# Two-layer graph network on one core: the down product's three terms in one 256-column sum, with two sets of PSUM banks

## What is computed

```
h = relu(layernorm(x));  s = h @ W.T
x1 = x + segment_sum(s[dst] * edge_weight, src)
h = relu(layernorm(x1))
g = h + segment_sum(h[src], dst)
h1 = g @ W1 + b1                      # 256 -> 1024
h1 = relu(batchnorm(h1))              # mean, variance over all rows
out = x1 + relu(h1 @ W2 + b2)         # 1024 -> 256
```

## Time and profile before

| what | value |
|---|---|
| median of 3 runs | 3991.4 us (3989.78 to 3992.15) |
| profiled execution | 3991.25 us, of which 3989.1 us from its first to its last instruction |
| mean granted clock of TensorE | 0.946 |
| TensorE busy | 3528.1 us (88%) |
| VectorE busy | 2164.4 us (54%) |
| ScalarE busy | 2165.5 us (54%) |
| GpSimd busy | 1029.7 us (26%) |

### The profile page before, as it was taken

One profiled execution on the slowest core, in us unless ns is written; L12 is line 12 of the kernel. 1 busy time (PEld: TensorE's weight loads), 2 busy tenths in 40 slices (PEclk: granted clock), 3 DMA queues, 4 the chain that ended last, 5 costly groups with the idle time before them and its releaser, 6 DMA issues.

```text
span 3989.1 us, 58593 instructions
## 1 busy us (share of the span) xinstructions
PE 3528.1 (88%) x17911; PEld 3007.3 (75%) x17911; DVE 2164.4 (54%) x5128; ACT 2165.5 (54%) x3631; POOL 1029.7 (26%) x801
## 2 busy tenths in 40 slices
PE   0477876688787689999999999999999999999999
PEld 0377776577666567778888888888888888888888
DVE  0466665476565578845555455455455555545544
ACT  0355554233322299946666656666666666665665
POOL 6288888688877700000000000000000000000000
PEclk9888888788888899999999999999999999999999
DMA  9977776577777799812212212211211221221220
GB/s 340 308 188 193 184 195 131 138 168 165 160 159 154 155 350 359 330 42 74 68 63 68 74 63 64 78 63 63 79 63 63 73 69 63 69 73 63 64 78 32
DMA packets 172581, 517.35 MB, mean 130 GB/s; under 512 B 26133, under 2 KB 78352, under 8 KB 166576
## 3 DMA queue, kind: packets, MB, share of 16 engines
q1 hardware_dynamic: 96160, 412.93, 30.0%
q0 software_dynamic: 75264, 102.81, 15.4%
q10 hardware_dynamic: 1072, 0.76, 0.1%
HBM read 361.58 MB, written 206.03 MB: 142 GB/s over the span
## 4 chain that ended last, share of the span: by engine, by line
PE 59%; POOL 19%; issue 9%; DMA 7%; ACT 5%; DVE 1%; ACTq 0%; POOLq 0%; SPq 0%; DVEq 0%
PE ps_a L1208 27%; PE ps_b L1222 18%; PE ps_b L1223 9%; POOL x_table L496 7%; POOL agg_table L496 6%; POOL arena L486 6%; DMA x_table<-in_x 4%; ACT arena L625 4%; PE ps_a L1192 2%; DMA agg_table<-arena,scatter_now 1%; DMA x_table<-arena,scatter_now 1%; ACT arena_r L643 1%; PE ps_b L1119 0%; DMA arena<-x_table,gather_ids 0%; PE ps_b L1108 0%
## 5 line engine op out<-in xcount | busy, mean ns | idle before, releaser
L1208 PE MATMUL ps_a<-arena_r 128*128 128x512 f32 (+1 forms) x4704 | 1198.3, 393 | 1.5 <-DVE arena_r L1031 1.5
L1222 PE MATMUL ps_b<-arena_r 128*128 128x512 f32 x3128 | 1138.1, 399 | 0.1
L1039 DVE TENSOR_TENSOR arena_r<-arena,arena_r 128x512 fp32r<-128x512 f32 (+1 forms) x784 | 540.2, 689 | 960.4 <-ACT arena_r L682 960.4
L677 ACT ACTIVATE arena<-ps_a,bn_bias,bn_scale 128x512 f32<-128x512 f32 (+1 forms) x784 | 607.2, 774 | 779.8 <-PE ps_a L1208 779.6
L1208 PEld LDWEIGHTS ps_a<-arena_r 128*128 128x128 f32 x4704 | 835.8, 188 | 178.7 <-ACT arena_r L668 1.9
L1223 PE MATMUL ps_b<-arena_r 128*128 128x256 f32 x3128 | 875.5, 280 | 0.0
L1222 PEld LDWEIGHTS ps_b<-arena_r 128*128 128x128 f32 x3128 | 587.8, 188 | 132.5 <-issue 0.4
L1223 PEld LDWEIGHTS ps_b<-arena_r 128*128 128x128 f32 x3128 | 590.5, 189 | 26.8
L682 ACT ACTIVATE arena_r<-arena 128x512 fp32r<-128x512 f32 (+1 forms) x784 | 495.0, 631 | 71.8 <-ACT arena L677 0.4
L1119 PE MATMUL ps_b<-arena,arena_r 128*128 128x256 f32 x1568 | 410.6, 428 | 0.0
L625 ACT ACTIVATE arena<-arena,norm_now 128x256 f32<-128x256 f32 (+1 forms) x782 | 405.2, 595 | 3.5 <-DVE norm_now L930 3.5
(11 more groups left out here) (116 smaller groups left out, 3879.2 us busy)
## 6 DMA issues: line engine op xcount, KB each, us to landing
arena<-x_table SPq DMA_DIRECT2D x291, 512.0 KB, 3.7
arena<-agg_table SPq DMA_DIRECT2D x194, 512.0 KB, 5.2
x_table<-in_x SPq DMA_DIRECT2D x10, 5000.0 KB, 32.5
agg_table<-zeros SPq DMA_DIRECT2D x40, 1250.0 KB, 5.3
out<-zeros SPq DMA_DIRECT2D x97, 512.0 KB, 6.0
arena<-in_x,gather_ids POOLq DMA_INDIRECT x196, 5.1
x_table<-arena,scatter_now POOLq DMA_INDIRECT x196, 4.0
arena<-x_table,gather_ids POOLq DMA_INDIRECT x196, 2.9
```

The source lines that it names most:

```text
L677: act.activation(hid[m % 2][:, 0:w], ps_a[:, 2 + m % 2, 0:w], ACT.Relu, scale=bn_scale[:, m:m + 1], bias=bn_bias[:, m:m + 1]).then_inc(hid ...
L1039: dve.tensor_tensor(hid_lo[m % 4][:, 0:w], hid[m % 2][:, 0:w], hid_hi[m % 4][:, 0:w].bitcast(F32), ALU.subtract).then_inc(hid_lo_ready, 1)
L1208: ins = pe.matmul(ps_a[:, 2 + m % 2, 0:w], w_part[:, kb, cols], h_part[:, kb, 0:w], start=(t == 0), stop=(t == len(terms) - 1))
L1222: pe.matmul(ps_b[0:p, r, :], hid_hi[m % 4][:, cols], w2, start=(m == 0), stop=(m == MB - 1), skip_group_check=True)
```

## The change

Each row group's sum now has 256 columns, and all three terms go into the same ones, in three matmuls of 256 columns where there was one of 512 and one of 256. Two groups share a bank. A chunk so needs two banks, and chunks take turns with two sets of two. Down block 0 waits until the sums of the chunk before the last have been read. VectorE reads the sums once, in two operations, and adds the bias; the operation that adds the second half goes, and with it a wait on VectorE's own counter. Down block 7 is no longer split: it stands whole behind up 0, and the semaphore of its first half goes.

The diff, without the declaration of the semaphore, the first increment of down_read by one before the loops, the counts of finish, and the length of VectorE's own counter in its loop (2 x LOADS to 0):

```diff
+        def node_sums(s, r):
+
+            return ps_b[:, 2 * s + r // 2, r % 2 * D:(r % 2 + 1) * D]
...
-                for half, rows in enumerate(halves(j)):
-                    if half == 0:
-                        dve.wait_ge(down_half, n + 1)
-                    else:
-                        dve.wait_ge(down_done, MB * n + MB)
-                    r0, r1 = rows[0], rows[-1] + 1
-                    chain.then(dve.tensor_tensor(out_sb[s][0:p, r0:r1, :], ps_b[0:p, r0:r1, 0:D],
-                                                 b2_bc[0:p, :].rearrange("p (a d) -> p a d", a=1).to_broadcast([p, r1 - r0, D]), ALU.add))
-                    chain.wait()
-                    dve.tensor_tensor(out_sb[s][0:p, r0:r1, :], out_sb[s][0:p, r0:r1, :], ps_b[0:p, r0:r1, D:2 * D],
-                                      ALU.add).then_inc(down_read, 1)
+                dve.wait_ge(down_done, MB * n + MB)
+                for r0, r1 in ((0, 2), (2, j)):
+                    ins = dve.tensor_tensor(out_sb[s][0:p, r0:r1, :],
+                                            ps_b[0:p, 2 * s + r0 // 2, 0:(r1 - r0) * D].rearrange("p (a d) -> p a d", d=D),
+                                            b2_bc[0:p, :].rearrange("p (a d) -> p a d", a=1).to_broadcast([p, r1 - r0, D]), ALU.add)
+                ins.then_inc(down_read, 1)
...
-            def down(n, m, half=None):
+            def down(n, s, m):
...
                 if m == 0 and not (isinstance(n, int) and n == 0):
-                    pe.wait_ge(down_read, 2 * n)
-                w2 = w2_hl[:, m, :, :].rearrange("p t d -> p (t d)")
-                for r in (range(j) if half is None else halves(j)[half]):
+                    pe.wait_ge(down_read, n)
+                for r in range(j):
                     cols = slice(r * p, (r + 1) * p)
-                    pe.matmul(ps_b[0:p, r, :], hid_hi[m % 4][:, cols], w2, start=(m == 0), stop=(m == MB - 1), skip_group_check=True)
-                    ins = pe.matmul(ps_b[0:p, r, 0:D], hid_lo[m % 4][:, cols], w2[:, 0:D], start=False, stop=(m == MB - 1), skip_group_check=True)
-                ins.then_inc(down_half if half == 0 else down_done, 1)
+                    for i, (rows, part) in enumerate(((hid_hi, 0), (hid_hi, 1), (hid_lo, 0))):
+                        ins = pe.matmul(node_sums(s % 2, r)[0:p, :], rows[m % 4][:, cols], w2_hl[:, m, part, :],
+                                        start=(m == 0 and i == 0 and r % 2 == 0), stop=(m == MB - 1 and i == 2), skip_group_check=True)
+                ins.then_inc(down_done, 1)
...
-                    down(n - 1, MB - 2)
-                    down(n - 1, MB - 1, half=0)
+                    down(n - 1, (s - 1) % LOADS, MB - 2)
                 up(n, 0)
                 if not (isinstance(n, int) and n == 0):
-                    down(n - 1, MB - 1, half=1)
+                    down(n - 1, (s - 1) % LOADS, MB - 1)
```

More of the change, by code:

```diff
@@ L257, in gnn_program @@
         hid_lo_ready = sem("hid_lo_ready")
-        down_half = sem("down_half")
         down_done = sem("down_done")
@@ L880, in _ @@
             dve.sem_inc(gram_lo, 2)
+            dve.sem_inc(down_read, 1)
             dve.wait_ge(consts_ready, 3)
@@ L1005, in read_down @@
                 dve.wait_ge(out_retired, n + 1)
-                for half, rows in enumerate(halves(j)):
-                    if half == 0:
-                        dve.wait_ge(down_half, n + 1)
-                    else:
-                        dve.wait_ge(down_done, MB * n + MB)
-                    r0, r1 = rows[0], rows[-1] + 1
-                    chain.then(dve.tensor_tensor(out_sb[s][0:p, r0:r1, :], ps_b[0:p, r0:r1, 0:D],
-                                                 b2_bc[0:p, :].rearrange("p (a d) -> p a d", a=1).to_broadcast([p, r1 - r0, D]), ALU.add))
-                    chain.wait()
-                    dve.tensor_tensor(out_sb[s][0:p, r0:r1, :], out_sb[s][0:p, r0:r1, :], ps_b[0:p, r0:r1, D:2 * D],
-                                      ALU.add).then_inc(down_read, 1)
+                dve.wait_ge(down_done, MB * n + MB)
[4 more added lines that the diff above has]
+                ins.then_inc(down_read, 1)
             def finish(n, s):
                 p, j = shape_of(n)
-                dve.wait_ge(down_read, 2 * n + 2)
+                dve.wait_ge(down_read, n + 2)
                 dve.scalar_tensor_tensor(out_sb[s % 2][0:p, 0:j, :], out_sb[s % 2][0:p, 0:j, :], 0.0, x1_in[s][0:p, 0:j, :],
@@ L1046, in main @@
                         pick_norm(n + 2, s % 2)
-            main_schedule(dve, main, loop=lambda passes, body: looped(passes, 2 * LOADS, body))
+            main_schedule(dve, main, loop=lambda passes, body: looped(passes, 0, body))
             read_down(CHUNKS - 1, (CHUNKS - 1) % 2)
@@ L1236, in main @@
                     up(n, m)
-                    down(n, m - 2)
+                    down(n, s, m - 2)
             main_schedule(pe, main)
-            down(CHUNKS - 1, MB - 2)
-            down(CHUNKS - 1, MB - 1, half=0)
-            down(CHUNKS - 1, MB - 1, half=1)
+            down(CHUNKS - 1, (CHUNKS - 1) % LOADS, MB - 2)
+            down(CHUNKS - 1, (CHUNKS - 1) % LOADS, MB - 1)
 def kernel(x, src, dst, edge_weight, L0_gnn_W, L1_gnn_W1, L1_gnn_b1, L1_gnn_gamma, L1_gnn_beta, L1_gnn_W2, L1_gnn_b2):
```

## The result

The changed kernel takes 4070.25 us (median of 4 runs, 4068.69 to 4072.71); the kernel before, run beside it, 3991.78 us. The ratio is 1.020 with a 95% interval of 1.0188 to 1.0212: 78 us slower. The forecast was 4061 us, with a range from 4018 to 4085. The profiled execution took 4072.71 us, 81.5 more than that of before; their spans are 4070.8 and 3989.1 us, 81.8 apart.

What follows compares the result with a forecast made beforehand. TensorE, busy throughout the main stage at full clock, was taken as the bound. Narrower down matmuls (+31 us) and the wait before up 0 (+39 us) added 70 us to 3991.4, giving 4061 us, range 4018 to 4085.

Steps and rivals of the forecast that it cites:

- Term 1: Main stage's down blocks: twelve 256-column matmuls take 1.435 us, 0.040 more than now; 782 x 0.040 = +31 us.
- U: The six matmuls of an up call on TensorE, read as 1.39 us.
- rival on the other side: Down blocks: a 256-column matmul costs its columns only, 0.107 us, giving 3959 us; chance 0.07.
- Term 2: Before up 0: TensorE arrives too early, waits 0.295 us plus 0.11 for the weight load; 96 x 0.405 = +39 us.
- chain: ScalarE, then VectorE's subtraction, prepare up 0's transposed h; up 0 could start at 3016.64, 0.35 us to spare before the change.
- bare weight load: At up 0: a weight load behind a wait isn't hidden, 0.11 us more a chunk.
- The slack before down 0: VectorE's low part of hidden block 0 done about 3021.7, down 0 wanting it at 3022.355: 0.65 us to spare.
- rival of a further wait: Down 0 waits too if reads or low part take 0.65 longer; up to 4130 us, chance 0.04.
- The clock: Main stage: clock expected still 1.00; rival that TensorE's pauses lower it, 4230 us, chance 0.03.
- The view of waits: Sign before up 0: TensorE waiting for VectorE's subtraction some 96 times, 0.3 us each, about 28 us in all.

Runs made afterwards that it cites:

- half of down 7 first in the new and in the old layout: New: changed kernel with half of down 7 before up 0, 4017.5 us; old: kernel before with 512-column down matmuls cut into two of 256, 4015.4 us.
- the wait halved: Changed kernel, up 0 waiting for the transposed rows' first half, then for the second before its last three matmuls: 4013.6 us, ratio 1.005.
- uneven cut: Kernel before, with the 512-column matmul of a down block cut into 384 and 128 columns: 4171.0 us, ratio 1.0444.

## Why the prediction was right, and where it was off

**The bound.** TensorE had no slack in the main stage, so nothing taken from VectorE and no wait taken from down 0 could gain. The kernels with half of down 7 first in the new and in the old layout, both at 23.40 us a chunk, show it: banks and reads are worth nothing between them.

**Term 1.** Forecast 0.040 a block and 31 us; measured 0.031 a block and 23 to 26 us (the two kernels above, and 0.25 us a chunk). Its price from the edge stage's stream, 0.1196 for a matmul of 256 columns, held: a block of twelve is 1.43 us. The term was mis-sized in both of its members by a few ns: the new block came out at 1.43, not 1.435, and the present one is 1.40 in the median over the stage, not the 1.395 that came from rounding U up to 1.39 and taking it from the pair. The rival on the other side, columns alone at 0.107, is excluded by the same rows. Whether the few ns are the price of the load or of the matmul itself was not told apart, as each narrow matmul brought both. The Trainium skill's "TensorE: Matmul & The Clock Gate", section "Back-to-back issue gap", has 109 ns for 256 columns, which gives 1.31 for the block as an estimate; the section itself says that this formula counts too little for small matmuls with loads, and the trace's 1.43 agrees with that.

**Term 2.** Forecast 0.405 a chunk and 39 us; measured 0.58 a chunk, 96 x 0.58 = 55 us (53 to 57 by the medians of the changed kernel and of those with the order restored or the wait halved). The mechanism was right: chain, arrival of TensorE at 2.30 us after the transposes, and the row of waits. The step that failed in size is the one "From the end of a VectorE result to TensorE's start takes 0.05": here it took 0.24. It was taken from a place where no instruction of the sequencer stands in the way; before up 0 there are two, and the order shown ahead of the prediction has two ISA rows there. With one it is 0.14. The bare weight load was forecast at 0.11 and is 0.09 (1.48 against 1.39). So 0.295 + 0.11 became 0.49 + 0.09.

The two sizes missed in opposite ways, some 6 us too many in the one and 16 too few in the other. That the sum of 70 came within 9 us of the measured 78 is in part luck.

**The slack before down 0.** Forecast 0.65 to spare on VectorE; the changed kernel has 3023.63 - 3023.04 = 0.59, of which some 0.5 can be used, and doubling the reads turned it into a wait of 0.67. The rival of a further wait was so the right thing to fear, and the kernel with wide matmuls in the new order ran into it.

**The clock.** The granted clock was 1.00 in every stretch of the main stage, with pauses of about 0.5 us in 24. The section "A second HAM failure mode: psum-queue depth-cycling" of that page of the Trainium skill tells of a kernel in which short idle times between groups of matmuls made the clock go up and down; no row here shows that.

**The view of waits.** It gave 29.8 us in 89 rows, near the 28 forecast, while the loss was over 50, so this agreement is an accident: a record of a matmul runs on for some 0.16 us after the next could start, so a short hole reads shorter than it is, and what the restart costs stands in the length of the next block. The lengths between starts have it all.

## What to carry to other kernels

On an engine without slack, count instructions and not only columns: a matmul of 256 columns with a weight load of its own cost 0.1195 us where half of one of 512 costs 0.116, and one of 128 columns still cost about 0.11. Work that stands between a producer chain and its consumer is cover; before you move it, write down how much of it the chain needs, or let the consumer wait only for the part that its first instructions read. Write the wait that comes last behind the others, so that no instruction stands between it and the one that needs it; one such instruction was worth 0.10 us here.

## What the runs showed of the hardware that was not expected

In a stream with a load of 128 weight columns before each matmul, one of 128 columns cost about 0.11 us (uneven cut, 0.40 us a row group against 0.359 by columns, 1.63 against 1.43 a block), the same 0.112 as one of 2 columns in the edge stage. With two instructions of the sequencer behind VectorE's recorded end, TensorE started 0.24 us after it, with one 0.14.
